# Attention of a transformer layer written out without its loop, its value blocks in two parts; the output projection's normalised inputs formed one half batch ahead

## The chip, the core and the metric

The kernel runs on one core of a Trainium2 chip. The core has five engines with instruction queues of their own: TensorE (PE, matmuls, with its weight loads shown as PEld), VectorE (DVE), ScalarE (ACT), GpSimd (POOL) and SyncE (SP), which here only issues transfers. They share an on-chip memory (SBUF), the accumulators of TensorE (PSUM, eight banks of 512 float32 values in each of 128 partitions) and 16 DMA engines to the chip's main memory. Engines wait for each other by semaphores. The metric is the device time of one execution in microseconds (us); lower is better.

## What is computed

A whole layer on 8 batches of 1024 tokens with 256 features: a gated linear attention with residual, then a block with softmax attention and a mixture of experts. The change touches the softmax attention and what follows it up to the router. Of the reference:

```python
def _attention(x, wq, wk, wv, wo, num_heads=16):
    ...
    scores = jnp.einsum('bqhd,bkhd->bhqk', q, k) * scale
    probs = jax.nn.softmax(scores, axis=-1)
    out = jnp.einsum('bhqk,bkhd->bqhd', probs, v).reshape(B, S, H)
    return out @ wo.T

def _moe(x, gate_w, w1, w2, w3):
    ...
    logits = xf @ gate_w.T
    rw, sel = jax.lax.top_k(logits, TOP_K)
    rw = jax.nn.softmax(rw.astype(jnp.float32), axis=-1).astype(x.dtype)
    ...
h = x + _attention(_rmsnorm(x, ln1_w), wq, wk, wv, wo)
h = h + _moe(_rmsnorm(h, ln2_w), gate_w, w1, w2, w3)
```

Sixteen heads of 16 features; S is 1024, H is 256, eight experts, two chosen for each token.

## The kernel before

Six stages run one after the other, with a barrier between them: gla_and_projections (the linear attention and the q, k, v projections), softmax_attention, output_projection_and_gate, route_and_transpose_weights, experts and combine. Each writes what the next needs to main memory.

**softmax_attention** works on 64 pairs of heads. The q and k of a pair lie in 64 partitions per head (50 used: high and low parts, and two rows for the maximum), so a matmul of one head uses one half of TensorE's rows, and two of different heads can run at once. A pair is done in 8 steps, one per block of 128 keys (kt). A step has

- four scores matmuls (head 0, queries 0 to 511 and 512 to 1023, then head 1), 128 keys by 512 queries each, into one of three PSUM banks p_e in turn (EB is 3). Each waits until ScalarE has emptied the bank (e_done).
- four exponentials on ScalarE, one for each (line 755), into probs. Four probs buffers hold two steps. The maximum of each query is already in the scores, through the two extra rows of q.
- four half maxima matmuls for the pair two ahead (max_half, line 838): scores once more, queries in the partitions, 1024 keys in p_m. Two halves make a unit, and VectorE reduces it with one reduce_max (line 816). Two p_m buffers, one unit for each head.
- one value block (values, line 852) for the step before: v and a column of ones as weights, 32 columns wide, so that the four (head, half of the queries) lie beside each other in four column tiles; probs is the moving operand, 512 wide, in float32, which the hardware does in two passes. Row 16 of every tile gives the sum of the exponentials. p_o adds up over the 8 steps.

TensorE's order in a step is: scores 0, maxima unit (2 halves), scores 1, maxima unit, scores 2, values of the step before, scores 3. In step 2 (NEG_AT) the transpose of the next pair's maxima stands between scores 2 and the values (max_transpose); ScalarE negates it (line 739) and SyncE writes it into the two rows of q (line 715). Behind step 0's exponentials ScalarE copies p_o of the pair before to oT (evacuate, line 745), the values of step 1 wait for that, and GpSimd stores oT to o_d (line 787). All engines run a hardware loop (Fori) over 15 groups of four pairs (RING) and then the last four written out; semaphore thresholds in the loop come from registers. The last two pairs have no maxima to form.

**output_projection_and_gate** works on 16 halves of a batch, 512 tokens each. For a half, SyncE loads the sums (den_in, row 16 of o_d), VectorE inverts them (line 1064), ScalarE stores the inverses to rd_d, SyncE loads them back spread over 16 partitions (rd, line 968) beside the unnormalised output (oin, line 961) and the residual inputs (xy, line 995). VectorE multiplies oin and rd into oT (normalised, line 1072), TensorE projects (line 1166), VectorE adds xy twice (h, line 1106, and base, line 1110), ScalarE and GpSimd form the root mean square, VectorE scales to xg (line 1119), TensorE transposes xg (line 1149), ScalarE scales the transpose (line 1023), TensorE does the router (line 1156) and VectorE chooses the experts (choose, lines 1083 to 1096). Transposes, router and choice run one half behind. VectorE's order in a half n: invert sums of n+2, h and base of n, choose n-1, normalise n+1, xg of n.

## Time and profile before

| what | us |
|---|---|
| median of three runs | 3438.69 |
| lowest and highest | 3434.74, 3439.25 |
| the profiled execution, its own time | 3437.48 |
| its span | 3435.9 |
| attention, from its first memset to the last copy | 795.1 to 2214.4 |
| output projection and gate | 2223.4 to 2464.4 |

The profile is of one execution. Its page gives each engine's busy time, the busy share in 40 slices, the granted clock of TensorE and the costliest groups of instructions. The busy share of TensorE over attention is 1385 of 1419 us, but its matmuls are recorded with their pipeline, so that a busy TensorE need not be one at its peak. The timeline of a short window is the better view: each row is one instruction or a run of like ones (x4), with start, length, engine, line, and in brackets how long the engine had been idle and what ended that. "64*128" before the shape of a matmul is the tiling of the array: 64 rows by 128 columns; the values use 128*32.

### The profile page before, as it was taken

To read this page: it belongs to the slowest core of one execution; us is meant where nothing else is said; L and a number is where in the kernel's file an instruction comes from. 1 tells how busy PE (TensorE), PEld (TensorE's weight loads), DVE (VectorE), ACT (ScalarE), POOL (GpSimd) and SP (SyncE) were. 2 spreads that over 40 slices of the span, in tenths; PEclk is the share of its full clock that TensorE was granted. 3 is DMA by queue.
4 is the path that set the end of the run, shared out by engine and by line. 5 is a ranking of instruction groups with operands and counts; after the bars stand their busy time and mean duration, and the time that the engine had idled before them with its cause. 6 is when DMAs were issued, how large, how long until landed. Compare 5 with 4: busy or idle time off the path is not lost. (4 is left out here: it accounts for less than half of the span.)

```text
span 3435.9 us, 64564 instructions
## 1 busy us (share of the span) xinstructions
PE 2978.2 (87%) x18668; PEld 1894.2 (55%) x18669; DVE 2315.4 (67%) x3776; ACT 1836.9 (53%) x3407; POOL 613.2 (18%) x974
## 2 busy tenths in 40 slices
PE   5888888876999999999999999666577999999970
PEld 4666666653444444444444444255466888888860
DVE  5677777646888888888888888244594444444436
ACT  3555555530888888888888888622142333333320
POOL 1212222210000000000000000000133444444430
PEclk7999999975999999999999999977688999999995
DMA  1332232322222222222222222177431111111129
GB/s 35 111 110 99 98 102 100 108 99 83 63 66 64 64 64 63 65 64 63 63 63 63 63 63 63 35 235 238 132 116 37 50 49 49 50 49 50 49 62 367
DMA packets 194561, 297.57 MB, mean 87 GB/s; under 512 B 31656, under 2 KB 117952, under 8 KB 194512
## 3 DMA queue, kind: packets, MB, share of 16 engines
q1 hardware_dynamic: 148688, 218.81, 20.3%
q0 software_dynamic: 18176, 52.45, 4.6%
q10 hardware_dynamic: 27648, 25.69, 2.5%
q8 instruction: 26, 0.43, 0.0%
q14 instruction: 23, 0.19, 0.0%
HBM read 167.28 MB, written 127.40 MB: 86 GB/s over the span
## 5 line engine op out<-in xcount | busy, mean ns | idle before, releaser
L816 DVE TENSOR_REDUCE b_mxq<-b_p_m 128x1 f32<-128x1024 f32 x1024 | 1205.9, 1219 | 159.9 <-PE b_p_m L838 159.8
L755 ACT ACTIVATE b_probs<-b_p_e 128x512 f32<-128x512 f32 x2048 | 1065.9, 605 | 283.5 <-PE b_p_e L877 277.2
L877 PE MATMUL b_p_e<-b_qst,b_kst 64*128 64x512 f32 x2048 | 643.9, 472 | 6.7 <-ACT b_probs L755 6.7
L838 PE MATMUL b_p_m<-b_kst,b_qst 64*128 64x512 f32 x2048 | 608.4, 423 | 28.6 <-DMA b_vst<-v_d 23.6
L852 PE MATMUL b_p_o<-b_probs,b_vst 128*32 128x512 f32 x4104 | 546.6, 605 | 0.7 <-ACT b_probs L755 0.7
L877 PEld LDWEIGHTS b_p_e<-b_qst,b_kst 64*128 64x128 f32 x2048 | 251.2, 184 | 507.5 <-ACT b_probs L755 416.3
L838 PEld LDWEIGHTS b_p_m<-b_kst,b_qst 64*128 64x128 f32 x2048 | 341.9, 189 | 180.6 <-DVE b_mxq L816 130.0
L1456 ACT ACTIVATE d_act<-d_p_up 128x512 f32<-128x512 f32 x136 | 81.2, 597 | 494.4 <-PE d_p_up L1518 494.4
L787 POOL DMA_DIRECT2D o_d<-b_oT x64 | 36.2, 566 | 1292.8 <-ACT b_oT L745 1292.8
L1533 PE MATMUL d_p_y<-w2T,d_hT 128*128 x1096 | 258.7, 379 | 0.8 <-ACT d_hT L1450 0.8
L1518 PE MATMUL d_p_up<-up_hi,d_xh 128*128 x544 | 250.2, 460 | 5.3 <-DVE d_xl L1475 1.5
L1471 DVE TENSOR_SCALAR d_xh<-d_p_x,d_ln 128x128 fp32r<-128x128 f32 x272 | 82.9, 346 | 246.2 <-PE d_p_x L1512 246.2
L1533 PEld LDWEIGHTS d_p_y<-w2T,d_hT 128*128 128x128 f32 x1096 | 207.3, 189 | 34.9 <-issue 1.0
L1518 PE MATMUL d_p_up<-up_lo,d_xh 128*128 x544 | 215.9, 397 | 0.0
L1518 PE MATMUL d_p_up<-up_hi,d_xl 128*128 x544 | 214.5, 394 | 0.0
L1423 POOL DMA_INDIRECT ys_d<-d_y,d_code x136 | 135.8, 998 | 295.4 <-DVE d_y L1482 291.2
L1411 POOL DMA_INDIRECT d_xs<-xg_d,d_tok x136 | 134.8, 991 | 116.2 <-POOL d_tok L1408 109.4
L1482 DVE COPY d_y<-d_p_y 128x256 f32<-128x256 f32 x137 | 58.1, 424 | 144.0 <-PE d_p_y L1533 144.0
L1166 PE MATMUL c_p<-c_woT,c_oT 128*128 128x256 f32 x256 | 100.3, 576 | 54.4 <-DVE c_oT L1072 54.4
L852 PEld LDWEIGHTS b_p_o<-b_probs,b_vst 128*32 128x32 f32 x4104 | 80.8, 108 | 120.6 <-issue 74.6
L1518 PEld LDWEIGHTS d_p_up<-up_hi,d_xh 128*128 128x128 f32 x544 | 102.9, 189 | 33.4 <-issue 18.3
L1166 PEld LDWEIGHTS c_p<-c_woT,c_oT 128*128 128x128 f32 x256 | 76.5, 306 | 73.5 <-DVE c_oT L1072 50.8
(254 smaller groups left out, 4071.9 us busy)
## 6 DMA issues: line engine op xcount, KB each, us to landing
b_qst<-qk_d SPq DMA_DIRECT2D x384, 64.0 KB
b_kst<-qk_d SPq DMA_DIRECT2D x384, 64.0 KB
x1y_d<-a_x1y SPq DMA_DIRECT2D x32, 512.0 KB, 4.1
qk_d<-a_hi SPq DMA_DIRECT2D x32, 512.0 KB, 2.8
qk_d<-a_lo SPq DMA_DIRECT2D x32, 512.0 KB, 3.7
v_d<-a_v_s SPq DMA_DIRECT2D x16, 1024.0 KB, 6.9
b_vst<-v_d SPq DMA_DIRECT2D x64, 256.0 KB
o_d<-b_oT POOLq DMA_DIRECT2D x64, 256.0 KB, 2.6
```

Source lines behind the costliest of these rows:

```text
L755: nc.scalar.activation(probs[e // 2 % 4][:, (e % 2) * 512:(e % 2 + 1) * 512], p_e[(slot(e) if more1 else e) % EB][:], ACT.Exp, scale=SCALE ...
L816: V_.reduce_max(mxq[half][:, h, qt:qt + 1], p_m[j % 2][:], AX.X).then_inc(s["m_red"], 1)
L838: mm(p_m[j % 2][:, kh * 512:(kh + 1) * 512], qst[r][rows(h), qt * P:(qt + 1) * P], kst[r][rows(h), kh * 512:(kh + 1) * 512], start=True, s ...
L852: last = mm(p_o[32 * (2 * h + a):32 * (2 * h + a) + 32, :], vst[r if kt >= 0 else (r - 1) % RING][:, kt % KT, h, :], probs[(2 * kt + h) % ...
L877: mm(p_e[u % EB][:], kst[r][rows(h), kt * P:(kt + 1) * P], qst[r][rows(h), a * 512:(a + 1) * 512], start=True, stop=True).then_inc(s["e_ps ...
L1166: i = mm(p2[:, t // 2, (t % 2) * D:(t % 2 + 1) * D], oT[half][:, k, t * P:(t + 1) * P], woT[:, k, :], start=(k == 0), stop=(k == 1))
L1411: g.indirect_dma_start(xs[r][:], None, xg_d, bass.IndirectOffsetOnAxis(ap=tok[r][:, 0:1], axis=0)).then_inc(s[f"x_in{r}"], 16)
L1423: g.indirect_dma_start(ys_d, bass.IndirectOffsetOnAxis(ap=code[r][:, 0:1], axis=0), y[r][:], None).then_inc(s[f"y_out{r}"], 16)
L1456: nc.scalar.activation(act_s[r][:], p_up[r][:, 0], ACT.Silu).then_inc(s["act_done"], 1)
L1471: last = V_.tensor_scalar(xh[r][:, k], p_x[:, k], ln2[:, k:k + 1], None, ALU.mult)
L1518: last = mm(p_up[r][:, u], x[r][:, k], w[:, bass.ds(e, 1), u, k, :].rearrange("p o n -> p (o n)"), start=(j == 0), stop=(j == 5))
L1533: last = mm(p_y[:, 0:D], hT[r][:, k], w2T[:, bass.ds(e, 1), k, :].rearrange("p o n -> p (o n)"), start=(k == 0), stop=(k == 3))
```

## The change

Attention (softmax_attention):

- The loop over pairs is written out for all 64, all thresholds are constants. The helper semaphore turn goes.
- A step is now two equal halves: scores, a maxima unit (two halves), scores, and one part of the values of the step before. A part is 256 queries wide (of each 512), so it has as many matmuls as the whole block had, each half as wide. In step 1 both parts stand at the end of the step, behind the wait for the copy of p_o. In step 2 the transpose of the maxima stands ahead of the fourth scores.
- Behind the last pair SyncE loads the sums of the first seven batches from o_d, VectorE inverts them in one instruction (128x896) and SyncE stores them to rd_d.

Output projection: written out for all 16 halves. Only the last batch's sums are inverted there. oin and rd are loaded two halves ahead (behind oT_done of the half that frees the buffer), and VectorE normalises half n+1 at the head of half n's work. The first loads are ordered oin, rd, xy, weights, then oin and rd of half 1.

The core of the diff:

```diff
-        with eng.Fori(0, STEPS - 1) as i:
-            for r in range(RING):
-                body(i * RING + r, i, r, True, True, True)
-        for r in range(RING):
-            body((STEPS - 1) * RING + r, STEPS - 1, r, r < RING - 1, r < RING - 2, r < RING - 3)
+        for pair in range(PAIRS):
+            body(pair, pair // RING, pair % RING, pair < PAIRS - 1, pair < PAIRS - 2, pair < PAIRS - 3)
...
         pairs(sp, body)
+        sp.wait_ge(s["o_stored"], 16 * (PAIRS - 8))
+        for n in range(BEFORE):
+            sp.dma_start(den[:, n], o_sums[n // 2, n % 2, :, 16, :].rearrange("g (c j) -> g c j", c=8)).then_inc(s["den_in"], 16)
+        sp.wait_ge(s["den_done"], 1)
+        sp.dma_start(rd_d[0:n_batches - 1].rearrange("b a g (c j) -> (g c) (b a) j", c=8), den[:]).then_inc(s["den_out"], 16)
...
+        dve.wait_ge(s["den_in"], 16 * BEFORE)
+        V_.reciprocal(den[:], den[:]).then_inc(s["den_done"], 1)
...
+            at = 256 * part
             for h in range(2):
                 for a in range(2):
-                    last = mm(p_o[32 * (2 * h + a):32 * (2 * h + a) + 32, :], vst[r if kt >= 0 else (r - 1) % RING][:, kt % KT, h, :],
-                              probs[(2 * kt + h) % 4][:, a * 512:(a + 1) * 512], start=(kt == 0), stop=(kt == -1))
+                    last = mm(p_o[32 * (2 * h + a):32 * (2 * h + a) + 32, at:at + 256], vst[r if kt >= 0 else (r - 1) % RING][:, kt % KT, h, :],
+                              probs[(2 * kt + h) % 4][:, a * 512 + at:a * 512 + at + 256], start=(kt == 0 and part == 0), stop=(kt == -1), skip_group_check=True)
...
-            for kt in range(KT):
-                scores(kt, 0)
-                maxima(4 * kt)
-                scores(kt, 1)
-                maxima(4 * kt + 2)
-                scores(kt, 2)
...
+            for kt in range(KT):
+                for half in range(2):
+                    scores(kt, 2 * half)
+                    if more:
+                        max_half(pair + 2, r2, 4 * kt + 2 * half)
+                        max_half(pair + 2, r2, 4 * kt + 2 * half + 1)
+                    if 4 * kt + 2 * half == NEG_AT and more1:
+                        pe.wait_ge(s["e_done"], pair * SLOTS + (NEG_AT + 2))
+                        max_transpose(pair + 1, (NEG_AT + 1) % EB)
+                    scores(kt, 2 * half + 1)
...
+        def body(n, half, b, b_next, before, after):
+            if n + 2 < N:
+                sp.wait_ge(s["oT_done"], n + 1)
+                load_output(half, b + 1)
+                load_inverses(half, b + 1)
```

TensorE in attention, step 3 of the first pair, before (p_e0 to p_e2 are the scores' banks, p_m0 and p_m1 the maxima units, p_o the values; REGISTER_ALU works out a threshold):

```order
L876 REGISTER_ALU
L877 MATMUL b_p_e1<-b_qst0,b_kst0 128x512
L837 REGISTER_ALU
L838 MATMUL b_p_m0<-b_kst2,b_qst2 128x512 x2
L876 REGISTER_ALU
L877 MATMUL b_p_e2<-b_qst0,b_kst0 128x512
L837 REGISTER_ALU
L838 MATMUL b_p_m1<-b_kst2,b_qst2 128x512 x2
L876 REGISTER_ALU
L877 MATMUL b_p_e0<-b_qst0,b_kst0 128x512
L852 MATMUL b_p_o<-b_probs0,b_vst0 32x512 x2
L852 MATMUL b_p_o<-b_probs1,b_vst0 32x512 x2
```

TensorE in the same step after, in whole:

```order
L887 MATMUL b_p_e1<-b_qst0,b_kst0 128x512
L843 MATMUL b_p_m0<-b_kst2,b_qst2 128x512 x2
L887 MATMUL b_p_e2<-b_qst0,b_kst0 128x512
L860 MATMUL b_p_o<-b_probs0,b_vst0 32x256 x2
L860 MATMUL b_p_o<-b_probs1,b_vst0 32x256 x2
L887 MATMUL b_p_e0<-b_qst0,b_kst0 128x512
L843 MATMUL b_p_m1<-b_kst2,b_qst2 128x512 x2
L887 MATMUL b_p_e1<-b_qst0,b_kst0 128x512
L860 MATMUL b_p_o<-b_probs0,b_vst0 32x256 x2
L860 MATMUL b_p_o<-b_probs1,b_vst0 32x256 x2
```

The values were one block of eight behind three scores and two maxima units, with the fourth scores behind it (and after that the next step's first); they are now two blocks, each half as wide, each behind two scores and one maxima unit.

TensorE in step 2 of the first pair, from the last scores ahead of the transpose, before:

```order
L877 MATMUL b_p_e1<-b_qst0,b_kst0 128x512
L891 REGISTER_ALU
L841 REGISTER_ALU
L842 MATMUL b_p_e2<-b_ident,b_hl 32x128
L852 MATMUL b_p_o<-b_probs2,b_vst0 32x512 x2
L852 MATMUL b_p_o<-b_probs3,b_vst0 32x512 x2
L876 REGISTER_ALU
L877 MATMUL b_p_e0<-b_qst0,b_kst0 128x512
```

TensorE at the same place after, from the third scores on:

```order
L887 MATMUL b_p_e1<-b_qst0,b_kst0 128x512
L843 MATMUL b_p_m1<-b_kst2,b_qst2 128x512 x2
L847 MATMUL b_p_e2<-b_ident,b_hl 32x128
L887 MATMUL b_p_e0<-b_qst0,b_kst0 128x512
L860 MATMUL b_p_o<-b_probs2,b_vst0 32x256 x2
L860 MATMUL b_p_o<-b_probs3,b_vst0 32x256 x2
```

The transpose (line 842, now 847) stood directly ahead of the values; it now stands ahead of the fourth scores, which stand ahead of the values.

VectorE in the output projection, one half of the last batch, before:

```order
L1106 TENSOR_TENSOR c_h<-c_p2,c_xy0 128x1024
L1110 TENSOR_TENSOR c_base0<-c_h,c_xy0 128x1024
L1083 COPY c_lg<-c_p4 128x32
L1087 MAX c_top<-c_lg 128x8 x4
L1092 MAX_INDEX c_tidx<-c_top,c_lg 128x8 x4
L1094 COPY c_best<-c_top 128x8
L1096 CAST chosen<-c_tidx 128x8
L1072 TENSOR_TENSOR c_oT1<-c_oin1,c_rd1 128x1024
L1119 TENSOR_SCALAR c_xg0<-c_h,c_r_s 128x256 x4
```

VectorE after, a half of the second batch:

```order
L1054 TENSOR_TENSOR c_oT1<-c_oin1,c_rd1 128x1024
L1088 TENSOR_TENSOR c_h<-c_p2,c_xy0 128x1024
L1092 TENSOR_TENSOR c_base0<-c_h,c_xy0 128x1024
L1065 COPY c_lg<-c_p4 128x32
L1069 MAX c_top<-c_lg 128x8 x4
L1074 MAX_INDEX c_tidx<-c_top,c_lg 128x8 x4
L1076 COPY c_best<-c_top 128x8
L1078 CAST chosen<-c_tidx 128x8
L1099 TENSOR_SCALAR c_xg0<-c_h,c_r_s 128x256 x4
```

The normalised input of the next half (c_oT) stood behind the choice; it now stands ahead of the sums of the present half (c_h, c_base), and the choice lies behind both.

## Rows read from the trace of the kernel before

**Rows 1.** Timeline of TensorE, one step: start us, length us, engine, line, work
```profile
1122.25 0.50 PE L877 MATMUL b_p_e<-b_qst,b_kst 64*128 64x512 f32 x2
1122.58 0.39 PE L838 MATMUL b_p_m<-b_kst,b_qst 64*128 64x512 f32 x1
1122.59 0.39 PE L877 MATMUL b_p_e<-b_qst,b_kst 64*128 64x512 f32 x1
1122.82 0.97 PE L838 MATMUL b_p_m<-b_kst,b_qst 64*128 64x512 f32 x3
1123.43 0.49 PE L877 MATMUL b_p_e<-b_qst,b_kst 64*128 64x512 f32 x1
1123.85 1.07 PE L852 MATMUL b_p_o<-b_probs,b_vst 128*32 128x512 f32 x8
1124.85 0.50 PE L877 MATMUL b_p_e<-b_qst,b_kst 64*128 64x512 f32 x2
```

**Rows 2.** Timeline, a pair without maxima: third scores of two steps
```profile
2181.29 0.49 PE L877 MATMUL b_p_e<-b_qst,b_kst 64*128 64x512 f32 x1 [0.45 <-ACT b_probs L755]
...
2183.89 0.50 PE L877 MATMUL b_p_e<-b_qst,b_kst 64*128 64x512 f32 x1 [0.45 <-ACT b_probs L755]
```

**Rows 3.** Timelines of ScalarE and VectorE in the same steps as rows 1
```profile
1125.38 2.06 ACT L755 ACTIVATE b_probs<-b_p_e 128x512 f32<-128x512 f32 x4 [0.54 <-PE b_p_e L877]
...
1123.25 2.35 DVE L816 TENSOR_REDUCE b_mxq<-b_p_m 128x1 f32<-128x1024 f32 x2 [0.25 <-PE b_p_m L838]
```

**Rows 4.** Timeline, steps 1 and 2 of a pair, and step 1 of a later one
```profile
1112.46 0.58 ACT L745 COPY b_oT<-b_p_o 128x512 f32<-128x512 f32 x1
...
1113.09 1.06 PE L852 MATMUL b_p_o<-b_probs,b_vst 128*32 128x512 f32 x8
...
1115.83 0.28 PE L842 MATMUL b_p_e<-b_ident,b_hl 128*32 128x128 f32 x1
...
1116.04 1.06 PE L852 MATMUL b_p_o<-b_probs,b_vst 128*32 128x512 f32 x8
...
2110.12 1.06 PE L852 MATMUL b_p_o<-b_probs,b_vst 128*32 128x512 f32 x8
```

**Rows 5.** Timeline of the output projection, one half
```profile
2372.61 6.26 PE L1166 MATMUL c_p<-c_woT,c_oT 128*128 128x256 f32 x16 [3.18 <-DVE c_oT L1072]
2378.70 1.04 PE L1149 MATMUL c_p<-c_ident,c_xg 128*128 128x128 f32 x8
2381.09 1.95 PE L1156 MATMUL c_p<-c_gwT,c_xgT 128*128 128x8 f32 x16 [1.36 <-ACT c_xgT L1024]
...
2385.05 1.22 DVE L1072 TENSOR_TENSOR c_oT<-c_oin,c_rd 128x1024 f32<-128x1024 f32 x1 [0.15 <-issue]
```

**Rows 6.** Timeline of TensorE in stage one: column tiles, 256 wide
```profile
338.25 0.64 PE L586 MATMUL a_p_g<-a_Sbd,a_qh 128*32 128x256 f32 x8 [0.53 <-ACT a_v_s L252]
338.82 1.11 PE L589 MATMUL a_p_g<-a_V,a_AT 128*128 128x64 f32 x8
```

**Rows 7.** Timeline, first pair; then the code queue, 870 to 1000 us (transfers, MB)
```profile
858.50 1.06 PE L852 MATMUL b_p_o<-b_probs,b_vst 128*32 128x512 f32 x8
...
q8 instruction: 4, 0.07, 0.2%
```

**Rows 8.** Projection: timeline, then two windows (busy per engine, clock, DMA share, GB/s)
```profile
2223.44 1.30 SPq L957 DMA_DIRECT2D c_den_in<-o_d  x2
...
2232.09 0.29 PEld L1140 LDWEIGHTS c_p<-c_ident,c_wo_raw 128*128 128x128 f32 x2 [19.33 <-DMA c_ln<-in_L_ffn_ln_w_dram]
...
2239.08 6.44 PE L1166 MATMUL c_p<-c_woT,c_oT 128*128 128x256 f32 x16 [5.27 <-DVE c_oT L1072]
...
2440.64 6.37 PE L1166 MATMUL c_p<-c_woT,c_oT 128*128 128x256 f32 x16 [2.98 <-DVE c_oT L1072]
...
2263.10:2440.60 177.50, 117.90 (x520) 98.29 (x520) 85.67 (x299) 42.79 (x130) 16.46 (x26) 0.75 0.78 231
...
2374.00:2376.00 2.00, 2.00 (x6) 1.59 (x5) 0.06 (x1) 0.00 (x0) 0.00 (x0) 0.50 1.05 277
```

More of the change, by code:

```diff
@@ L877, in scores @@
                 mm(p_e[u % EB][:], kst[r][rows(h), kt * P:(kt + 1) * P], qst[r][rows(h), a * 512:(a + 1) * 512], start=True, stop=True).then_inc(s["e_ps"], 1)
-            def maxima(first):
-                if more:
-                    max_half(pair + 2, r2, first)
-                    max_half(pair + 2, r2, first + 1)
             for kt in range(KT):
-                scores(kt, 0)
-                maxima(4 * kt)
-                scores(kt, 1)
-                maxima(4 * kt + 2)
-                scores(kt, 2)
-                if 4 * kt + 2 == NEG_AT and more1:
-                    pe.wait_ge(s["e_done"], pair * SLOTS + (NEG_AT + 2))
-                    max_transpose(pair + 1, (NEG_AT + 1) % EB)
-                if kt == 1:
-                    pe.wait_ge(s["oT_done"], pair + 1)
-                values(r, kt - 1, pair * SLOTS + ((slot(4 * kt - 1) if more1 else 4 * kt - 1) + 4))
-                scores(kt, 3)
+                for half in range(2):
[7 more added lines that the diff above has]
+                    scores(kt, 2 * half + 1)
+                    read = pair * SLOTS + ((slot(4 * kt - 1) if more1 else 4 * kt - 1) + 4)
+                    if kt == 1 and half == 0:
+                        continue
+                    if kt == 1:
+                        pe.wait_ge(s["oT_done"], pair + 1)
+                        values(r, 0, 0, read)
+                    values(r, kt - 1, half, read)
         pairs(pe, body)
-        values(0, -1, PAIRS * SLOTS + 2)
+        for part in range(2):
+            values(0, -1, part, PAIRS * SLOTS + 2)
 def output_projection_and_gate(nc, ctx, o_d, rd_d, x1y_d, wo, gate_w, ln2_w, base_d, xg_d, chosen, share, n_batches=8):
@@ L1069, in normalised @@
             dve.wait_ge(s[f"rd{half}"], b * 32 + 32)
-            if before:
+            if n > 1:
                 dve.wait_ge(s["h_ps"], n - 1)
             V_.tensor_tensor(oT[half][:], oin[half][:], rd[half][:], ALU.mult).then_inc(s["oT_done"], 1)
-        for half in (0, 1):
-            inverses(half, half, 0)
+        normalised(0, 0, 0, False)
         dve.wait_ge(s["wT_ps"], 1)
@@ L1078, in _ @@
         V_.tensor_copy(gwT[:].rearrange("p k m -> p (k m)"), p1[:, 1, 0:2 * NE]).then_inc(s["wT_done"], 1)
-        normalised(0, 0, 0, False)
+        dve.wait_ge(s["sums_in"], 32)
+        V_.reciprocal(sums[:], sums[:]).then_inc(s["sums_done"], 1)
         def choose(n):
@@ L1096, in choose, with body @@
             V_.tensor_copy(chosen[:, bass.ds(n * T, T), :], tidx[:, :, 0:2]).then_inc(s["copied"], 1)
-        def body(n, half, b, b_next, before, after, after2):
+        def body(n, half, b, b_next, before, after):
             n1 = n + 1
-            if after2:
-                inverses(n + 2, half, b + 1)
+            if after:
+                normalised(n + 1, 1 - half, b_next, before)
             dve.wait_ge(s[f"in{half}"], b * 16 + 16)
@@ L1114, in body @@
                 choose(n - 1)
-            if after:
-                normalised(n + 1, 1 - half, b_next, before)
             dve.wait_ge(s["r_done"], n1)
@@ L1157, in router, with body @@
             i.then_inc(s["lg_ps"], 1)
-        def body(n, half, b, b_next, before, after, after2):
+        def body(n, half, b, b_next, before, after):
             n1 = n + 1
```

97 lines of the change are left out of this document (36 added, 61 removed).

## The prediction

> **What bounds the kernel now.** I read the page's slices first: two stretches are touched by the change, attention (795 to 2214 us of the span) and the output projection (2223 to 2464 us). Then I read the timeline of TensorE and ScalarE over one key block of attention, and of all engines over one half batch of the projection.
>
> Attention repeats a step (one of 8 key blocks) 8 times for each of 64 pairs of heads. TensorE looks busy all the time, but its step of 2.60 us [rows 1] is set elsewhere. The last two pairs have no maxima at all, and their step is 2.60 us too: from 2181.29 to 2183.89, where the row says that TensorE sat idle 0.45 us for an exponential [rows 2]. So neither the maxima matmuls nor VectorE set the step. The chain that closes is: third scores matmul, +0.42 us values, +1.00 us fourth scores [rows 1], +0.53 us its exponential starts, +0.60 us that ends (four take 2.06 us: 0.49 us from start to start, 0.60 to the end), then the bank is free for the next third scores, 0.05 us later [rows 3]. 0.42 + 1.00 + 0.53 + 0.60 + 0.05 = 2.60. With three banks, and with the fourth scores behind a whole value block, that is the loop. ScalarE idles 0.54 us and VectorE 0.25 us in each step [rows 3]. Two steps of a pair are longer. From 1113.09 to 2110.12 us lie 47 pairs: 21.21 us each. In step 2 a transpose is added: from the values of step 1 to those of step 2 are 2.95 us. That leaves 21.21 - 6 x 2.60 - 2.95 = 2.66 for step 1, where the values wait for the copy of the output [rows 4].
>
> The projection takes a half batch in 13.65 us (13 of them in the 177.5 us of the last view) [rows 8]. TensorE runs 6.1 us of projection for half n, 1.0 us of transposes and 1.95 us of router matmuls for half n-1, and then waits. The normalised input of half n+1 is formed by VectorE only at 2385.05 us, behind the choice of experts of half n-1, which waits for the router. So projection, transposes, router, choice, normalising and the next projection stand in one line, and round again [rows 5].
>
> **The change part by part.** *Value blocks in two parts, each behind a unit of maxima.* In the new order a step is twice: scores, two maxima matmuls, scores, half the values. The fourth scores no longer stand behind a whole value block, so the chain above opens, and TensorE's own time becomes the step. A half consists of three distances.
>
> First, from the first matmuls after the values to the second ones of the same rows: 1122.25 to 1122.58, 0.33 us. Both row groups take part (the scores use one, the maxima the other), as now. Second, from those to the values. Twice in [rows 1] the work in the other tiling starts 0.07 us before the recorded end of the last matmul (values at 1123.85 against 1123.43 + 0.49; scores at 1124.85 against 1123.85 + 1.07). The last matmuls of a half have had their weights loaded ahead and take 0.39 us, so 0.39 - 0.07 = 0.32 us. Third, the half block: attention has none, but stage one runs the same form, 128x256 in four column tiles, eight matmuls, with the next work 0.57 us later [rows 6]. That is 1.22 us for a half and 2.44 for a step. I take 2.45.
>
> What runs beside it: exponentials 4 x 0.49 = 1.96 us, two reduces 2.35 us [rows 3]. VectorE's reduces are what comes next, so a step can't fall under 2.35. Slack of the other waits: the first half's values need the last exponential of the step before. The fourth scores start 1.55 us into a step, their exponential starts at 2.24, ends at 2.84, which is 0.39 into the next step; the values start at 0.65.
>
> *Step 1* keeps both parts together at its end. The fourth scores need the exponential of the first, which stands behind the copy of the output (0.58 us, of which 0.46 before the next can start) [rows 4]: the exponential of step 0's last scores starts at -0.20, the copy at 0.29, the exponential of the first scores 0.75 to 1.35, the fourth scores at 1.40, the values at 1.82, both parts 1.03. That is 2.85 us, 0.19 more than now. *Step 2* has the transpose now directly ahead of the values, in the same tiling. Afterwards it stands ahead of the fourth scores, so a change of tiling and back is added: third scores at 1.22, second maxima matmul 1.55, transpose 1.87, fourth scores 0.21 later (as the values now follow it, 1115.83 to 1116.04), values 0.42 later, next step 0.57 later: 3.07 us, against 2.95 now.
>
> A pair: 6 x 2.45 + 2.85 + 3.07 = 20.62 us against 21.21, 0.59 less. Over 62 to 63 pairs that is -36 us.
>
> Here the notes speak against the change. Each value part costs two changes of tiling, and [rows 1] show about 0.15 us of idle array before the values and 0.22 after. The Trainium skill, in "TensorEngine Tiling (Array Packing)", section Key Properties, says that switching the mode drains the engine. By that rule a second pair of switches costs 0.37 us a step; the rows agree, and the 2.44 above already holds it. It is paid out of the 0.5 us that the open chain frees.
>
> *No loop.* PAIRS bodies are written out. Register arithmetic ahead of TensorE's waits goes; no row shows it to cost anything, and I take nothing for it. Code now streams from memory: some 390 instructions per pair, 1.5 blocks of 16 KB. The first pass through the old loop loads code as well, 4 blocks in 870 to 1000 us, and costs nothing: from the first evacuated value block at 858.50 to 1113.09 are 12 pairs of 21.22 us [rows 7]. I take 0 for it. Issue is no bound either: the half block of stage one is 8 matmuls and 8 weight loads in 0.57 us, 36 ns each [rows 6]; a new step has 24 and 24 in 2.45 us, 51 ns each.
>
> *Sums of the rows.* 14 small loads, one reciprocal and one store move into the tail of attention, to SyncE and VectorE, which have nothing left to do in the last two pairs (42 us). SyncE issues a load of this kind in 0.65 us [rows 8], 9 us in all; VectorE took 0.55 us for 64 columns, so some 8 us for 896. With the store some 22 us lie beside 42: free, and were the cover gone, those 22.
>
> *The projection.* The normalised input of half n+1 is formed at the head of half n's work, the loads run two halves ahead, and the sums' round trip through memory is gone for all but the last batch. TensorE's line is then projection 5.9, transposes to router 2.4, router 1.95, next projection: 2372.61 to 2383.04, 10.4 us, and less if it stays warm: over the stretch its granted clock was 0.75 [rows 5, 8]. The next bound is the DMA engines. 231 GB/s over 13.65 us are 3.15 MB a half; the small loads take 0.06 off. Where the queues are full they moved 277 GB/s at a share of 1.05 [rows 8], so 3.09 MB take 11.1 us; by the mean share, 0.78 x 13.65 = 10.6. I take 10.7, from both bounds. Now the first projection starts at 2239.08 us, 15.6 into the stage, behind the round trip of the sums. The weights' transposes start at 2232.09, since their load is queued behind 2 MB, and that stays; they and the copies end at 2234.7. The stage from there to the last projection: 15 x 10.7 = 160.5 us from 2234.7 ends at 2395.2, against 2440.64 [rows 8]. That is -45 us; what follows the last projection stays.
>
> **Sum.** The profiled execution has a span of 3435.9 us and took 3437.5; the median of the three runs is 3438.7. 3438.7 - 36 - 45 = 3358 us.
>
> **Rivals.** *A: the switches cost more than I take.* Place: last scores to values, twice a step. The only distance measured in attention is 0.42 us, not 0.32. If it holds whatever the matmul ahead, a half takes 0.10 more, a pair (15 such places) 20.62 + 1.5 = 22.12, so 0.91 x 62.5 = +57 us, and with the projection's -45 the kernel takes 3451, slower. It decides from a half of 1.31 us. For it: no row shows values behind paired matmuls. Against: the 0.49 us matmul ahead of the values waits for its own weights. *B: attention gains nothing* (a half of 1.26 us or stalls in steps 1 and 2): 3394. *C: the DMA engines don't reach their peak*, 12.3 us a half: 3438.7 - 36 - 21 = 3382. *D: both go better*: steps of 2.38, just over VectorE's 2.35, a pair 20.12, -68 us; 9.5 us a half, -63: 3308. *E: row groups don't overlap in the new order.* In [rows 1] a scores matmul starts at 1122.59, before the second maxima matmul at 1122.82 that precedes it in the program. If it had to queue, each of the 15 would take 0.24 us more, +3.6 us a pair: some 3580. The Trainium skill, "TensorE: Matmul & The Clock Gate", Part 3, has this order as strict. The trace shows otherwise. *F: streamed code stalls TensorE*, 2 us on each of about 96 blocks: some 3550. [Rows 7] speak against it.
>
> **Chances.** Forecast (3335 to 3385) 0.55; B 0.17; C 0.06; D 0.09; A 0.06; E 0.02; F 0.02; between B and A 0.03. A difference under 0.2%, 7 us, can't be told from none in this kernel. Faster: 0.55 + 0.17 + 0.06 + 0.09 = 0.87; same 0.03; slower 0.10. The range leaves out A, E, F and the outer part of D: 3312 to 3408.
>
> **What would show it.** In attention's timeline: steps of 2.44 us with values 0.32 us behind the second matmuls and 0.57 long; step 1 at 2.85, step 2 at 3.07; VectorE nearly without idle time. In the projection: normalising ahead of the sum of half n, projections 10.7 us apart with the DMA share near 1, TensorE waiting for inputs or warm throughout. Wrong it would be if values follow at 0.42 us, if idle time "issue" stands on TensorE at block borders, or if projections come 13 us apart.

## The result

The changed kernel takes 3359.66 us (median; 3358.72 to 3364.05) against 3438.43 (3434.74 to 3439.25): a ratio of 0.9775, with a 95% interval from 0.9759 to 0.9792. The forecast was 3358. The number is right to 2 us, but two terms of its sum were too large, and 7 us of the gain were in no term at all. The traces of the two executions (spans 3435.9 and 3358.6 us) show it by stage:

| what | before, us | after, us | difference | forecast |
|---|---|---|---|---|
| start to the first copy of p_o | 857.9 | 857.2 | -0.6 | 0 |
| first to last copy of p_o (64 pairs) | 1355.9 | 1323.6 | -32.3 | -36 |
| last copy to the last projection | 226.9 | 190.3 | -36.6 | -45 |
| last projection to the route stage | 25.0 | 24.0 | -1.0 | 0 |
| route stage to the experts' first gather | 133.0 | 133.8 | +0.8 | 0 |
| experts, first to last gather | 718.2 | 711.0 | -7.2 | 0 |
| from there to the end | 119.1 | 118.7 | -0.4 | 0 |

The differences add up to the 77.3 us by which the spans differ.

**Attention.** First the timeline of TensorE, half of a regular step of the changed kernel (start us, length us, engine, line, work). It answers to [rows 1].

```profile
1134.64 0.49 PE L887 MATMUL b_p_e<-b_qst,b_kst 64*128 64x512 f32 x1
1134.65 0.49 PE L843 MATMUL b_p_m<-b_kst,b_qst 64*128 64x512 f32 x1
1134.98 0.39 PE L887 MATMUL b_p_e<-b_qst,b_kst 64*128 64x512 f32 x1
1134.98 0.39 PE L843 MATMUL b_p_m<-b_kst,b_qst 64*128 64x512 f32 x1
1135.30 0.64 PE L860 MATMUL b_p_o<-b_probs,b_vst 128*32 128x256 f32 x8
1135.87 0.49 PE L887 MATMUL b_p_e<-b_qst,b_kst 64*128 64x512 f32 x1
```

A half is 0.34 + 0.32 + 0.57 = 1.23 us, and no row of TensorE in the window carries a wait. The scores and the maxima matmuls run side by side in their row groups. VectorE and ScalarE, which had gaps of 0.25 and 0.54 us in every step in [rows 3], have none that the timeline shows in the regular steps (first VectorE, then ScalarE):

```profile
1132.95 13.59 DVE L819 TENSOR_REDUCE b_mxq<-b_p_m 128x1 f32<-128x1024 f32 x11 [0.65 <-PE b_p_m L843]
```

```profile
1133.94 6.00 ACT L759 ACTIVATE b_probs<-b_p_e 128x512 f32<-128x512 f32 x10
```

Neither is the bound: the eleven reduces start 1.24 us apart, where two on end started 1.13 apart in [rows 3], and the exponentials start 0.60 apart against 0.49. With no wait on TensorE in the window, what is left is TensorE's own line.

Steps 1 and 2 of a pair, which answer to [rows 4]: ScalarE's copy of p_o, then TensorE.

```profile
1126.50 0.59 ACT L749 COPY b_oT<-b_p_o 128x512 f32<-128x512 f32 x1
```

```profile
1126.23 0.49 PE L887 MATMUL b_p_e<-b_qst,b_kst 64*128 64x512 f32 x1
...
1127.65 0.49 PE L887 MATMUL b_p_e<-b_qst,b_kst 64*128 64x512 f32 x1
1128.07 1.07 PE L860 MATMUL b_p_o<-b_probs,b_vst 128*32 128x256 f32 x16
1129.07 0.50 PE L887 MATMUL b_p_e<-b_qst,b_kst 64*128 64x512 f32 x1
...
1130.97 0.28 PE L847 MATMUL b_p_e<-b_ident,b_hl 128*32 128x128 f32 x1
1131.18 0.50 PE L887 MATMUL b_p_e<-b_qst,b_kst 64*128 64x512 f32 x1
1131.61 0.64 PE L860 MATMUL b_p_o<-b_probs,b_vst 128*32 128x256 f32 x8
1132.18 0.50 PE L887 MATMUL b_p_e<-b_qst,b_kst 64*128 64x512 f32 x1
```

Step 1 is 1126.23 to 1129.07, 2.84 us; step 2 is 1129.07 to 1132.18, 3.11 us; with six steps of 2.46 a pair is 20.71. The copies bear it out: from 1126.50 to this one are 47 pairs of 20.71.

```profile
2100.02 0.59 ACT L749 COPY b_oT<-b_p_o 128x512 f32<-128x512 f32 x1
```

The DMA view of 1000 to 2000 us shows the streamed code, 73 blocks in 48.3 pairs, 1.5 a pair. It answers to [rows 7]:

```profile
q8 instruction: 73, 1.20, 0.5%
```

The sums of the rows are done long before the last value block (timelines of SyncE, VectorE and TensorE):

```profile
2149.24 8.96 SPq L734 DMA_DIRECT2D b_den<-o_d  x14
2165.52 0.40 SPq L736 DMA_DIRECT2D rd_d<-b_den  x1
```

```profile
2159.74 5.75 DVE L831 RECIPROCAL b_den<-b_den 128x896 f32<-128x896 f32 x1 [20.26 <-DMA b_den<-o_d]
```

```profile
2179.69 1.07 PE L860 MATMUL b_p_o<-b_probs,b_vst 128*32 128x256 f32 x16 [0.37 <-ACT b_probs L759]
```

**Projection.** The start of the stage, a half early in it, and two late ones (TensorE, then VectorE and SyncE); these answer to [rows 5] and [rows 8].

```profile
2204.93 0.69 PE L1120 MATMUL c_p<-c_ident,c_wo_raw 128*128 128x128 f32 x2 [24.18 <-DMA c_ln<-in_L_ffn_ln_w_dram]
...
2233.27 5.39 PE L1146 MATMUL c_p<-c_woT,c_oT 128*128 128x256 f32 x16
2238.49 1.04 PE L1129 MATMUL c_p<-c_ident,c_xg 128*128 128x128 f32 x8
2240.88 1.95 PE L1136 MATMUL c_p<-c_gwT,c_xgT 128*128 128x8 f32 x16 [1.36 <-ACT c_xgT L1014]
...
2360.62 5.50 PE L1146 MATMUL c_p<-c_woT,c_oT 128*128 128x256 f32 x16 [3.61 <-DVE c_h L1088]
```

```profile
2355.30 1.22 DVE L1054 TENSOR_TENSOR c_oT<-c_oin,c_rd 128x1024 f32<-128x1024 f32 x1 [2.88 <-issue]
2359.25 1.23 DVE L1088 TENSOR_TENSOR c_h<-c_p,c_xy 128x1024 f32<-128x1024 f32 x1 [2.73 <-DMA c_xy<-x1y_d]
```

```profile
2250.72 5.40 SPq L961 DMA_DIRECT2D c_oin<-o_d  x2
2256.17 4.41 SPq L968 DMA_DIRECT2D c_rd<-rd_d  x2
2260.63 1.17 SPq L989 DMA_DIRECT2D c_xy<-x1y_d  x1
```

The normalised input now stands 4 us ahead of the sum (2355.30 against 2359.25). TensorE waits for the sum h, whose bank it needs, and the sum waits for the residual inputs xy. SyncE issues xy last, and the four issues ahead of it take 9.8 us. The window from the first projection to the last (length, busy per engine, clock, DMA share, GB/s) has 15 distances of 10.91 us in the mean. They are not alike: the first four are 9.1 us in the mean, the last eleven 11.6, and single ones lie between 7.2 and 12.9, where the kernel before had a steady 13.65.

```profile
2207.50:2371.14 163.64, 121.20 (x577) 102.06 (x577) 88.81 (x297) 46.24 (x141) 17.85 (x28) 0.81 0.86 278
```

**Experts.** Neither code nor order of this stage is changed. Its gathers (lengths in ns, first and last start) and TensorE's first weight load behind a border of its loop over four tiles, in the kernel before and then in the changed one:

```profile
L1411 POOL DMA_INDIRECT d_xs<-xg_d,d_tok x136: 971/990/1131, 2598.6 to 3316.8; - x136
...
2671.31 0.19 PEld L1518 LDWEIGHTS d_p_up<-up_hi,d_xh 128*128 128x128 f32 x1 [0.52 <-issue]
```

```profile
L1391 POOL DMA_INDIRECT d_xs<-xg_d,d_tok x136: 971/990/1131, 2528.9 to 3239.9; - x136
...
2601.74 0.19 PEld L1498 LDWEIGHTS d_p_up<-up_hi,d_xh 128*128 128x128 f32 x1 [0.27 <-issue]
```

The same load is issued 0.52 us late in one kernel and 0.27 in the other. The loop has 33 rounds: 33 x 0.25 = 8.2 us, about the 7.2 of the table. The gathers say the same more closely: a round takes 21.277 us before and 21.061 after, 7.1 us over 33.

### The profile page after: what moved, and what is told of

Its sections match the earlier page's. It is cut to its first block and busy times, and to the rows that moved or that the text cites. A ratio compares the mean times of both kernels' runs of the same rounds, so it can differ in the third digit from the quotient of the medians.

```text
span 3358.6 us, 64285 instructions
## 1 busy us (share of the span) xinstructions
PE 2939.7 (88%) x22780; PEld 1824.2 (54%) x22781; DVE 2353.8 (70%) x3762; ACT 1885.9 (56%) x3407; POOL 613.3 (18%) x974
## 5 line engine op out<-in xcount | busy, mean ns | idle before, releaser
L819 DVE TENSOR_REDUCE b_mxq<-b_p_m 128x1 f32<-128x1024 f32 x1024 | 1242.8, 1224 | 92.5 <-PE b_p_m L843 84.4
L759 ACT ACTIVATE b_probs<-b_p_e 128x512 f32<-128x512 f32 x2048 | 1113.7, 601 | 202.4 <-PE b_p_e L887 83.0
L843 PE MATMUL b_p_m<-b_kst,b_qst 64*128 64x512 f32 x2048 | 758.0, 452 | 28.6 <-DMA b_vst<-v_d 23.5
L887 PE MATMUL b_p_e<-b_qst,b_kst 64*128 64x512 f32 x2048 | 762.2, 447 | 1.0 <-ACT b_probs L759 1.0
L860 PE MATMUL b_p_o<-b_probs,b_vst 128*32 128x256 f32 x8208 | 642.5, 390 | 0.4 <-ACT b_probs L759 0.4
L887 PEld LDWEIGHTS b_p_e<-b_qst,b_kst 64*128 64x128 f32 x2048 | 310.6, 184 | 433.0 <-ACT b_probs L759 363.6
L860 PEld LDWEIGHTS b_p_o<-b_probs,b_vst 128*32 128x32 f32 x8208 | 168.1, 108 | 346.0 <-issue 217.7
L843 PEld LDWEIGHTS b_p_m<-b_kst,b_qst 64*128 64x128 f32 x2048 | 307.2, 188 | 60.3 <-DVE b_mxq L819 36.5
L1498 PEld LDWEIGHTS d_p_up<-up_hi,d_xl 128*128 128x128 f32 x544 | 102.4, 188 | 25.3
L1498 PEld LDWEIGHTS d_p_up<-up_lo,d_xh 128*128 128x128 f32 x544 | 103.5, 190 | 14.3
```

The lines of the kernel that those rows point to most:

```text
L759: nc.scalar.activation(probs[e // 2 % 4][:, (e % 2) * 512:(e % 2 + 1) * 512], p_e[(slot(e) if more1 else e) % EB][:], ACT.Exp, scale=SCALE ...
L819: V_.reduce_max(mxq[half][:, h, qt:qt + 1], p_m[j % 2][:], AX.X).then_inc(s["m_red"], 1)
L843: mm(p_m[j % 2][:, kh * 512:(kh + 1) * 512], qst[r][rows(h), qt * P:(qt + 1) * P], kst[r][rows(h), kh * 512:(kh + 1) * 512], start=True, s ...
L860: last = mm(p_o[32 * (2 * h + a):32 * (2 * h + a) + 32, at:at + 256], vst[r if kt >= 0 else (r - 1) % RING][:, kt % KT, h, :], probs[(2 * ...
L887: mm(p_e[u % EB][:], kst[r][rows(h), kt * P:(kt + 1) * P], qst[r][rows(h), a * 512:(a + 1) * 512], start=True, stop=True).then_inc(s["e_ps ...
L1498: last = mm(p_up[r][:, u], x[r][:, k], w[:, bass.ds(e, 1), u, k, :].rearrange("p o n -> p (o n)"), start=(j == 0), stop=(j == 5))
```

## Experiments

Stage times are compared rather than whole times where a stage is the question: the first copy of p_o comes between 852 and 864 us in the different executions, and the stage ahead of it is the same in all. The kernel before took 3435.57 us beside old_attention, unrolled_whole, values_at_end and transpose_late, 3435.56 beside copy_later, xy_first, no_base_store and weights_early, and 3438.21 beside the others; each ratio is to its own.

**Which half brings what.** old_attention puts attention's loop, step order and value blocks of before into the changed kernel. Its stage times are from old_attention_look, the same kernel run again for its profile.

```diff
-        for pair in range(PAIRS):
-            body(pair, pair // RING, pair % RING, pair < PAIRS - 1, pair < PAIRS - 2, pair < PAIRS - 3)
+        with eng.Fori(0, STEPS - 1) as i:
+            for r in range(RING):
+                body(i * RING + r, i, r, True, True, True)
```

> The changed kernel with attention's loop, step order and whole value blocks of before; the sums' inverses in attention's tail and the new output projection stay. If the gains add up (attention 32.9 us from the copies' rows, projection 37.6 up to the end of the stage), it takes 3359.7 + 33 = 3393 us, with a pair of 21.21 us and projections 10.9 us apart. If the projection's gain had needed attention's new order, or the experts stage's 7 us belong to one of the two, it comes out elsewhere: the experts stage takes 718 us from its first gather to its last with before's code placement, 711 with the changed kernel's; no theory says yet which this kernel has, so 3393 or 3400.

> The kernel old_attention again, for its profile: the time of 3390.6 us is 45 us under before, of which the projection stage explains 37.6. So the experts' border should stand at 0.26 to 0.31 us and that stage take 711 to 713 us, with attention's pair at 21.21 us. If the stage takes 718 us, the 7 us are elsewhere.

Measured: 3390.55 us, ratio 0.9873 (0.9857 to 0.9890), 45 us under before. A pair is 21.21 us, the projections are 10.86 us apart (2245.55 to 2408.50), and the experts stage takes 710.8 us (2566.2 to 3277.0) with its border at 0.26. (The repetition, a single execution of 3397.61 us, is 7 us longer than the first one's median; its first copy of p_o comes at 864.1 us, 6 later than in the kernel before.) The gains add up, and the experts' 7 us are there without any change in attention.

old_projection is the other half: attention changed, the output projection of before.

```diff
-            if after:
-                normalised(n + 1, 1 - half, b_next, before)
             dve.wait_ge(s[f"in{half}"], b * 16 + 16)
...
                 choose(n - 1)
+            if after:
+                normalised(n + 1, 1 - half, b_next, before)
```

> The changed kernel's attention (loop written out, values in two parts, without the sums' tail) with the output projection of before, loop and order and all. If the gains add up, the time up to the projection is 32.9 us shorter and the projection takes what it took: 3435.6 - 33 = 3403 us if the experts stage stays at 718 us (its weight load at the loop's border 0.52 us late, as before), 3395 if the experts stage takes 711 (0.26 us). The projection's loop is in it again, so this also tells whether it is attention's written out code or the projection's that moves the experts' border.

Measured: 3397.57 us, ratio 0.9885 (0.9869 to 0.9900). Pair 20.71 us; last copy to last projection 225.6 us (2182.7 to 2408.3), as before; experts stage 710.4 us, border 0.26. So either half alone moves the experts' border. The two single gains, 45.0 and 40.6, are 7 us more than both together, since that one is in each.

**Loop or order.** unrolled_whole writes attention out, but keeps the order and the whole value blocks of before.

```diff
-                for half in range(2):
-                    scores(kt, 2 * half)
...
-                    values(r, kt - 1, half, read)
+                scores(kt, 0)
+                maxima(4 * kt)
...
+                values(r, kt - 1, pair * SLOTS + ((slot(4 * kt - 1) if more1 else 4 * kt - 1) + 4))
+                scores(kt, 3)
```

> The changed kernel, attention without its loop, but with the step order and the whole value blocks of before. If writing out the loop is free (the prediction's term), a pair takes 21.21 us as before and the kernel 3393 us, the same as with the loop. Rival: register arithmetic ahead of TensorE's waits cost something, then a pair is shorter than 21.21 (0.1 us a step would give 20.4 and 3340). Rival: streamed code stalls, then a pair is longer than 21.21 at some borders (each 2 us on 96 blocks is 3 us a pair).

Measured: 3389.15 us, ratio 0.9863 (0.9846 to 0.9879). The pair is 21.13 us, so writing out is worth 0.08 a pair, 5 us in all. Regular steps are 2.60 us as with the loop; the 0.08 lie in the first three steps, and I did not follow them further. Of the pairs with maxima one took 21.37 us and the others 21.13 to 21.18, so streamed code can have cost 0.24 us once, and nowhere more. Of the 32.3 us, 4.6 are the loop's (1351.3 instead of 1355.9 from the first copy to the last) and 27.7 the order's.

**The chain or the changes of tiling.** values_at_end keeps the new halves but puts both value parts behind the fourth scores in all steps, as step 1 has it.

```diff
-                    if kt == 1 and half == 0:
+                    if half == 0:
                         continue
...
-                    values(r, kt - 1, half, read)
+                    for part in range(2):
+                        values(r, kt - 1, part, read)
```

> The changed kernel with both value parts behind the fourth scores in every step: one change of tiling to the values and one back per step instead of two and two. If the chain of exponentials sets a step (first scores, 0.53 until its exponential starts, 0.60 until it ends, 0.05 until the fourth scores, 0.42 to the values, 1.00 for them) it is 2.60 us as before, a pair 7 x 2.60 + 2.85 = 21.0 to 21.3 us, the kernel some 3385 to 3395. Rival: the changes of tiling set it (0.15 + 0.22 us each pair of them), then a step is 2.46 - 0.37 = 2.1, which VectorE's two reduces hold at 2.38, a pair 20.0, the kernel some 3320.

Measured: 3408.98 us, ratio 0.9923 (0.9902 to 0.9944), pair 21.45. The expected range was 3385 to 3395, so the time is a miss by some 14 us; the step is not. Timelines of TensorE and ScalarE, one step:

```profile
1125.83 0.50 PE L887 MATMUL b_p_e<-b_qst,b_kst 64*128 64x512 f32 x1
1126.26 1.07 PE L860 MATMUL b_p_o<-b_probs,b_vst 128*32 128x256 f32 x16
1127.26 0.49 PE L887 MATMUL b_p_e<-b_qst,b_kst 64*128 64x512 f32 x1
...
1128.44 0.49 PE L887 MATMUL b_p_e<-b_qst,b_kst 64*128 64x512 f32 x1
```

```profile
1127.79 2.07 ACT L759 ACTIVATE b_probs<-b_p_e 128x512 f32<-128x512 f32 x4 [0.54 <-PE b_p_e L887]
```

From fourth scores to fourth scores are 2.61 us: 0.43 to the values, 1.00 for them, 0.53 until the first exponential starts, 0.60 until it ends, 0.05. That is the chain of the kernel before, link by link, with half as many changes of tiling as the changed kernel. The chain theory stands; fewer changes bring nothing while it is closed. The missing time lies in step 2, which the expectation took for a regular one: from the values of step 1 (1112.73) to those of step 2 (1115.83) are 3.10 us. The fourth scores behind the transpose start at 1115.41, after 0.20 us of waiting for an exponential. With 2.70 for step 1 and six of 2.61 that makes 21.46.

**A change of tiling where the chain is open.** transpose_late moves step 2's transpose behind the fourth scores, next to the values, whose tiling it has.

```diff
-    NEG_AT = 10
+    NEG_AT = 11
...
-                    if 4 * kt + 2 * half == NEG_AT and more1:
-                        pe.wait_ge(s["e_done"], pair * SLOTS + (NEG_AT + 2))
-                        max_transpose(pair + 1, (NEG_AT + 1) % EB)
                     scores(kt, 2 * half + 1)
+                    if 4 * kt + 2 * half + 1 == NEG_AT and more1:
+                        pe.wait_ge(s["e_done"], pair * SLOTS + (NEG_AT + 2))
+                        max_transpose(pair + 1, (NEG_AT + 1) % EB)
```

> The changed kernel with the transpose of the maxima directly ahead of step 2's second value part (behind the fourth scores) instead of ahead of the fourth scores: same tiling as the values, so one change of tiling and back less. By the rows (0.33 to the second matmuls, 0.33 to the transpose, 0.21 to the values, 0.57 for them) step 2 is 1.23 + 0.33 + 0.33 + 0.21 + 0.57 = 2.67 us instead of 3.11; a pair 20.27, 0.44 less, over 63 pairs -28: 3332 us. Rival: the exponential of the bank that the transpose takes (the second scores') comes last, or ScalarE's negation now delays the next exponentials: then step 2 stays near 3.1, or step 3 takes what step 2 gives: 3355 to 3360.

Measured: 3334.37 us, ratio 0.9699 (0.9683 to 0.9715), pair 20.29. TensorE in step 2, from its first scores to the next step's:

```profile
1124.84 0.50 PE L887 MATMUL b_p_e<-b_qst,b_kst 64*128 64x512 f32 x1
...
1126.40 0.39 PE L887 MATMUL b_p_e<-b_qst,b_kst 64*128 64x512 f32 x1
1126.41 0.39 PE L843 MATMUL b_p_m<-b_kst,b_qst 64*128 64x512 f32 x1
1126.73 0.28 PE L847 MATMUL b_p_e<-b_ident,b_hl 128*32 128x128 f32 x1
1126.95 0.64 PE L860 MATMUL b_p_o<-b_probs,b_vst 128*32 128x256 f32 x8
1127.52 0.50 PE L887 MATMUL b_p_e<-b_qst,b_kst 64*128 64x512 f32 x1
```

Step 2 is 2.68 us instead of 3.11. With TensorE's own line as the bound, one change of tiling and back, and the fourth scores again beside a maxima matmul, are worth 0.43 us. The Trainium skill, "TensorEngine Tiling (Array Packing)", section Key Properties, says that a switch of mode drains the engine. The trace agrees so far as work in the other tiling starts only 0.07 us ahead of a recorded end (in the changed kernel's step 2 the values at 1131.61 against 1131.18 + 0.50), while matmuls of one tiling start 0.33 us apart at a recorded length of 0.49. Whether a switch costs time depends on what else bounds the step: with one pair of them a step took 2.61 us in values_at_end, with two pairs 2.46 in the changed kernel.

**The copy in step 1.** copy_later is transpose_late with ScalarE's copy of p_o one exponential later.

```diff
-                if e == 3:
+                if e == 4:
                     evacuate(pair, r % 2)
```

> The kernel transpose_late, and in addition ScalarE copies the output of the pair before behind the first exponential of step 1 instead of ahead of it. By the rows the fourth scores of step 1 then start 1.18 us into it (0.53 + 0.60 + 0.05), the copy ends at 1.02 + 0.59 = 1.61, the values start there and take 1.00: step 1 is 2.62 us instead of 2.85, a pair 20.06 instead of 20.29, over 63 pairs -14.5: 3320 us. Rival: what is late next in step 1 is the second exponential, which now stands behind the copy and which the first scores of step 2 wait for (the bank), or the gap opens in step 2: then nothing or a loss, 3334 to 3345.

Measured: 3323.12 us, ratio 0.9676 (0.9660 to 0.9692), pair 20.11. ScalarE's copy, then TensorE in step 1:

```profile
1114.08 0.58 ACT L749 COPY b_oT<-b_p_o 128x512 f32<-128x512 f32 x1
```

```profile
1113.06 0.49 PE L887 MATMUL b_p_e<-b_qst,b_kst 64*128 64x512 f32 x1
...
1114.24 0.50 PE L887 MATMUL b_p_e<-b_qst,b_kst 64*128 64x512 f32 x1
1114.72 1.07 PE L860 MATMUL b_p_o<-b_probs,b_vst 128*32 128x256 f32 x16
1115.72 0.50 PE L887 MATMUL b_p_e<-b_qst,b_kst 64*128 64x512 f32 x1
```

The fourth scores start 1.18 us into the step, as worked out; the values start at 1.66, 0.06 behind the end of the copy; the step is 2.66 us instead of 2.84. Copying p_o in two parts, to free the first part's columns earlier, was not tried: TensorE would write one half of the bank while ScalarE reads the other, with nothing to order them.

**What bounds the projection.** no_base_store takes bytes away, xy_first changes SyncE's order, weights_early the first loads. For scale: the changed kernel's projection ran unchanged in six more kernels (old_attention_look, unrolled_whole, values_at_end, transpose_late, copy_later, padded). With the changed kernel's own 180.6 us and 10.91, they take 178.3 to 182.2 us from the stage's first transfer to the last projection, at distances of 10.79 to 11.00 us.

no_base_store leaves out the store of base and fills its memory with zeros in attention instead.

```diff
-            act.dma_start(base_v[n], base[half][:]).then_inc(s[f"st{half}"], 16)
```

> The changed kernel without the store of base (h plus the second residual input) in the output projection, 0.5 MB of 3.07 MB a half; its buffer in memory is filled with zeros during attention instead, so the output leaves out that term. Only the projection's distance is of interest. If the DMA rate bounds it, 2.55 MB at 281 GB/s take 9.1 us, under TensorE's own line of 9.4: projections 9.4 us apart instead of 10.9, about -20 us in the stage. Rival: not the bytes but the chain through VectorE, GpSimd and the queue's order bounds it: projections stay near 10.9 us apart. The whole time isn't to be compared closely, since 8 MB more are written in attention: some 3335 to 3345 by the first theory, 3360 by the second.

Measured: 3363.85 us as a whole (0.9790, 0.9774 to 0.9806), which says nothing here because of the 8 MB written in attention. The window from the first projection to the last, 15 distances:

```profile
2220.56:2376.93 156.37, 120.36 (x576) 101.50 (x577) 88.64 (x297) 46.15 (x141) 17.75 (x28) 0.82 0.83 244
```

That is 10.42 us a half instead of 10.91, and 172.0 us from the stage's first transfer to the last projection instead of 180.6. Both are outside what the same projection does by itself, so bytes count. But a sixth of the bytes took only 0.49 us a half with it: the expectation had 9.4 us by the DMA rate and 10.9 by its rival, and the result is nearer the rival. The busy time of the DMA engines fell from 0.86 x 10.91 = 9.4 to 0.83 x 10.42 = 8.6 us a half, and their rate from 278 to 244 GB/s. The loads themselves grew slower. SyncE's queue (packets, MB, share of the engines' time), in the changed kernel's window and then in this one:

```profile
q1 hardware_dynamic: 15803, 30.67, 60.0%
q1 hardware_dynamic: 15816, 30.70, 68.7%
```

The same 30.7 MB took 60.0% of 163.6 us, 98 us, with the stores of base beside them, and 68.7% of 156.4 us, 107 us, without. So the stage isn't bound by its bytes over a fixed rate. It waits for its loads, and what sets their pace no run here shows.

```diff
+            if after:
+                sp.wait_ge(s["in_free"], n + 2)
+                sp.dma_start(xy[1 - half][:], x1y_v[n + 1]).then_inc(s[f"in{1 - half}"], 16)
             if n + 2 < N:
                 sp.wait_ge(s["oT_done"], n + 1)
                 load_output(half, b + 1)
                 load_inverses(half, b + 1)
-            if after:
-                sp.wait_ge(s["in_free"], n + 2)
-                sp.dma_start(xy[1 - half][:], x1y_v[n + 1]).then_inc(s[f"in{1 - half}"], 16)
```

> The changed kernel with the load of the residual inputs (xy of half n+1) ahead of the loads of the output and the inverses of half n+2 on SyncE, instead of behind them. In the changed kernel VectorE's sum waits for xy in most halves, and xy is issued 3 us after its buffer is free, behind loads whose issue takes 4.6 and 3.8 us. If the DMA engines' rate bounds a half (3.07 MB at 281 GB/s is 10.9 us), the order changes little: projections stay 10.6 to 10.9 us apart, 3355 to 3360 us. Rival: the place of xy in the queue bounds it and TensorE's own line is next (9.4 us from projection to projection in the early halves): up to -1.5 us a half, -20: 3340 us. On the other side: the output's load, now later, becomes what is waited for: 3365 or more.

Measured: 3357.88 us (0.9778, 0.9762 to 0.9795), not to be told from the changed kernel as a whole. From attention's last copy to the last projection are 185.8 us instead of 190.3, with a distance of 10.59 us:

```profile
2205.97:2364.88 158.91, 122.16 (x576) 102.83 (x577) 87.73 (x297) 46.13 (x141) 18.38 (x28) 0.81 0.84 285
```

The 185.8 us are 176.1 from the stage's first transfer, under the 178.3 to 182.2 of the unchanged order. The order is worth some 4 us, not the 20 that TensorE's own line would leave. The wait only moves: in these 15 halves VectorE stands idle 45.1 us ahead of normalising, where only the loads of oin and rd can hold it, against 31.6 us for xy and 21.5 ahead of normalising in the changed kernel. SyncE is busy issuing for 3.9 us a half instead of 7.9, so its issuing isn't what sets the distance.

```diff
         load_output(0, 0)
-        load_inverses(0, 0)
-        sp.dma_start(xy[0][:], x1y_v[0]).then_inc(s["in0"], 16)
         sp.dma_start(wo_raw[:], wo.rearrange("(k p) n -> p k n", p=P)).then_inc(s["w_in"], 16)
...
+        load_inverses(0, 0)
+        sp.dma_start(xy[0][:], x1y_v[0]).then_inc(s["in0"], 16)
```

> The changed kernel with the projection's weights loaded behind the first output load (as before the change), ahead of the inverses and of xy. The weights' transposes then come 8.7 us into the stage instead of 14.4 and the first projection some 11.5 us into it instead of 17.0. If transfers bound the stage, the halves behind it don't end earlier, since the same bytes must pass: within 2 us of 3360. Rival: the late first projection is lost time in full: 3354 us.

Measured: 3362.32 us (0.9793, 0.9777 to 0.9809). The weights' transposes start 7.8 us into the stage and the first projection 14.0 instead of 17.0 (it now waits for the inverses, not at 11.5 as I had expected), yet the last projection starts 183.2 us into it instead of 180.6. The distances between projections grew to 11.28 us (2199.13 to 2368.31) instead of 10.91, outside the 10.79 to 11.00 above: an earlier first projection is given back later.

**The experts' border.** padded shifts the code of the experts' loop.

```diff
+        for _ in range(6):
+            tr(p_x[:, 0, :], xs[0][:, 0:P], ident[:])
         input_transposes(0, 16)
```

> The changed kernel with six transposes more on TensorE ahead of the experts' loop (0.1 us each, their result is overwritten), which shift all code of that loop in memory and change nothing else. If the place of the loop's code sets how late the first weight load behind its border is issued (0.52 us in the kernel before, 0.26 in the changed one, 0.31 in unrolled_whole), that distance changes, and the experts stage with 33 borders takes between 711 and 719 us instead of 711.0: 3360 to 3368 us. Rival: something else than the code's place sets it: 0.26 and 3360 us as before the padding.

Measured: 3357.76 us (0.9772, 0.9756 to 0.9789), stage 712.2 us, the load at the border again 0.26 us late. This shift did nothing. In unrolled_whole, with other code ahead, the load is 0.31 us late and the stage takes 712.4. So the distance has had three values in kernels with the same experts' code, 0.52 only in the kernel before. That the code's place sets it is not shown, and the cause stays open.

**The best version.** best is copy_later with xy_first's order.

> transpose_late, copy_later and xy_first together. copy_later took 3323.1 us; xy_first took 4.5 us off the way from attention's last copy to the last projection (185.8 us instead of 190.3): 3318.6 us. Rival: xy_first's gain was within the spread of runs (its median is only 1.8 us under the changed kernel's): 3323.

Measured: 3318.54 us, ratio 0.9661 (0.9644 to 0.9678), some 40 us under the changed kernel (39 by the ratios); last copy to last projection 186.5 us, against 190.2 in copy_later. Its interval overlaps that of copy_later (0.9660 to 0.9692), so the last 4 us rest on the stage's rows alone.

## Why the prediction was right, and where it was not

- **The chain that sets the step: right.** values_at_end rebuilt it and got 2.61 us. In the changed kernel it is open.
- **Half of 1.22 us: right to 0.01.** 0.34 + 0.32 + 0.57 by the rows. The row from stage one for the value part (0.57) held exactly, and so did the 0.07 us by which work in the other tiling starts ahead of a recorded end. Rival A (0.42 us to the values) didn't occur, and E neither: a pair would have had 3.6 us more.
- **Steps 1 and 2: 2.84 and 3.11 us against 2.85 and 3.07.** The pair is 20.71 against 20.62: 0.06 from the six regular steps (2.46, not 2.45), the rest from step 2. Over 62.5 pairs that is 5.6 us too much gain in the sum; the last two pairs gave 1 us more than it held, so attention lacked some 4. The 0.15 and 0.22 us of idle array that the prediction reads beside a switch can be read off no row; what the runs show is the 0.43 us of transpose_late, for one pair of switches and the pairing of the fourth scores together.
- **VectorE as the next bound at 2.35: misread.** The row of two reduces, 2.35 us, is one distance from start to start (1.13) and one whole length (1.22). Two distances would be 2.3 us. Nothing in the sum hung on it, only rival D. That rival's pair of 20.12 us doesn't follow from its steps either: 6 x 2.38 + 2.85 + 3.07 is 20.20.
- **No loop, cost 0: nearly.** 5 us better, by unrolled_whole. Code came at 1.5 blocks a pair, as said, and rival F fell.
- **Sums in the tail: right.** Loads, reciprocal and store end by some 2168 us, before the last copy at 2181.
- **Projection, -45: too large, -37.6 with what follows.** The mean period was near, 10.91 us against 10.7, between the bounds of 10.6 and 11.1. Why it was near is in part luck: the prediction had a steady period at a DMA share near 1 and a rate that full queues give. The distances ran from 7.2 to 12.9 us at a share of 0.86. In no_base_store a sixth of the bytes less took off 4%, not 17%, and 277 GB/s is no ceiling, since xy_first moved 303 between 2234 and 2285.5 us. What failed is the step "their load is queued behind 2 MB, and that stays". In the kernel before, the weights stood behind the first 0.5 MB only; the change puts them behind 2 MB, as its own diff shows. So the first projection came 17.0 us into the stage, not 11.3. That and 15 x 0.21 us are the 8.8 us by which the stage up to the last projection (180.6 us) is over the 171.8 of the sum. The deeper fault is that the sum holds a start and a period as two terms that don't know of each other. In weights_early the start came 3 us earlier and the period grew by 0.37: where the stage waits for its loads, the two trade, and here only their sum was set. Undoing the 5.7 us would not have brought the forecast's -45.
- **Experts: in no step.** I took it that code which isn't edited keeps its time. It gave 7 of the 11 us that the two terms lacked, and so the forecast looks better than its steps were. Without it the kernel would have taken some 3367 us, still inside the range.

## What to carry to other kernels

When a wait closes a loop through two engines, add up its links from the rows and find the queue entry that stands in it needlessly; splitting that entry pays even if it doubles the changes of tiling, and once the chain is open each change of tiling is time of its own. In a stage that waits for its loads, a first start and a period can trade against each other, as in weights_early. Take its time from all of it, and don't price a transfer that you take away at its bytes over the mean rate: here it brought a quarter of that. Compare every stage of two traces, the untouched ones too, before a matching total is taken as proof.

## What the hardware showed that I had not expected

- The first weight load behind the border of an untouched loop was 0.52, 0.31 or 0.26 us late by issue in different kernels, 7 us over 33 rounds; one shift of the code by six matmuls did not change it.
- The DMA engines at a share of 0.83 to 0.86 moved 244, 278 or 285 GB/s in the stage. The last two are the same transfers in another order (changed kernel and xy_first), the first lacks the stores of base; the window of the kernel before at 0.78 had 231 [rows 8].
- Moving one 128x128 transpose next to work in its own tiling saved 0.43 us, more than its recorded length of 0.28 us.
